# One matmul of 129 columns for the high and low values of three query tiles, a semaphore for each weight tile, and five high halves in eight on ScalarE

## What is computed

```
wp, wo = row-normalised w_proj (1536 x 512), w_out (512 x 512), over sqrt(512)
h = wp @ x                                   # 1024 x 1536: per head q, k, v
q, k = pixnorm(q) * s, pixnorm(k) * s; v = pixnorm(v)
attn = softmax(q k^T over the 1024 keys)     # per head 1024 x 1024
res = attn @ v
out = (0.7 * x + 0.3 * (wo @ res)) / sqrt(0.58)
```

## Time and profile before

| | |
|---|---|
| median of 3 runs | 2988.52 us |
| the profiled execution, its own time | 2986.36 us |
| its span, first to last instruction | 2984.6 us |
| TensorE busy | 2933.4 us, 36928 matmuls |
| VectorE busy | 2581.7 us |
| ScalarE busy | 2383.4 us |
| GpSimd busy | 454.9 us |
| mean granted TensorE clock | 0.999 of full speed |

### The profile page before, as it was taken

The page is one execution under the profiler, slowest core; times in us unless marked ns, Lnnn a source line. Parts: engine busy times, 40 slices in busy tenths (PEclk is TensorE's granted clock), DMA queues, the critical chain, the costliest instruction groups (busy, mean ns, idle before and its releaser), DMA issues.

```text
span 2984.6 us, 85445 instructions
## 1 busy us (share of the span) xinstructions
PE 2933.4 (98%) x36928; PEld 2013.6 (67%) x36928; DVE 2581.7 (87%) x3197; ACT 2383.4 (80%) x2993; POOL 454.9 (15%) x678
## 2 busy tenths in 40 slices
PE   7999999999999999999999999999999999999998
PEld 5776666766667667676666766667666666666765
DVE  6898888988889888898888988888888888988887
ACT  6887878878778778787787877878787787878786
POOL 0210121101211112112111111012110121101210
PEclk9999999999999999999999999999999999999999
DMA  3133414333242332333323333223323334334234
GB/s 106 41 56 63 91 36 108 51 79 79 44 97 50 81 78 48 90 62 76 72 52 85 62 79 69 65 72 62 85 63 69 76 54 96 60 63 86 40 80 103
DMA packets 459529, 211.04 MB, mean 71 GB/s; under 512 B 407952, under 2 KB 407952, under 8 KB 459152
## 3 DMA queue, kind: packets, MB, share of 16 engines
q1 hardware_dynamic: 459152, 205.58, 32.3%
HBM read 71.30 MB, written 33.55 MB: 35 GB/s over the span
## 4 chain that ended last, share of the span: by engine, by line
PE 79%; DVE 8%; POOL 5%; ACT 3%; DMA 3%; issue 2%; SPq 0%; ACTq 0%; DVEq 0%
PE ps_pv L973 21%; PE ps_score L952 19%; PE ps_dense L930 11%; PE ps_dense L932 10%; PE ps_dense L934 10%; DVE probs L780 4%; PE ps_dense L989 3%; PE ps_dense L990 2%; PE ps_dense L991 2%; DMA x_raw<-in_x 2%; POOL rs_t L442 1%; POOL rs_t L444 1%; POOL rs_t L446 1%; ACT e_tile L596 1%; DVE probs L771 1%
## 5 line engine op out<-in xcount | busy, mean ns | idle before, releaser
L780 DVE TENSOR_TENSOR probs<-e_tile,probs 128x1024 f16<-128x1024 f32 x1024 | 1241.4, 1230 | 64.6 <-ACT probs L603 58.7
L596 ACT ACTIVATE e_tile<-ps_score,shift 128x1024 f32<-128x1024 f32 x1024 | 1107.9, 1118 | 223.7 <-PE ps_score L952 130.2
L973 PEld LDWEIGHTS ps_pv<-v_pair,probs 128*128 128x128 f16 x24576 | 772.2, 98 | 183.5 <-issue 112.4
L973 PE MATMUL ps_pv<-v_pair,probs 128*128 128x65 f16 (+1 forms) x24576 | 821.6, 193 | 2.9 <-DVE probs L780 1.7
L952 PE MATMUL ps_score<-qkT 64*128 64x512 f16 x6144 | 753.4, 378 | 3.3 <-ACT e_tile L596 3.1
L930 PE MATMUL ps_dense<-wpT_hi,x_hi 128*128 128x512 f32 x1536 | 621.0, 404 | 2.4 <-DVE wpT_lo L851 2.3
L932 PE MATMUL ps_dense<-wpT_lo,x_hi 128*128 128x512 f32 x1536 | 600.1, 391 | 0.0
L934 PE MATMUL ps_dense<-wpT_hi,x_lo 128*128 128x512 f32 x1536 | 599.0, 390 | 0.0
L603 ACT ACTIVATE probs<-e_tile 128x1024 f16<-128x1024 f32 x512 | 542.8, 1061 | 22.8 <-PE ps_pv L973 4.0
L952 PEld LDWEIGHTS ps_score<-qkT 64*128 64x128 f16 x6144 | 257.0, 94 | 361.4 <-issue 90.2
L771 DVE CAST probs<-e_tile 128x1024 f16<-128x1024 f32 x512 | 360.0, 703 | 72.0 <-PE ps_pv L973 67.6
(11 more groups left out here) (50 smaller groups left out, 1739.4 us busy)
## 6 DMA issues: line engine op xcount, KB each, us to landing
x_raw<-in_x SPq DMA_DIRECT2D x128, 256.0 KB, 3.4
x_res<-in_x SPq DMA_DIRECT2D x128, 256.0 KB, 3.6
out<-x_res SPq DMA_DIRECT2D x128, 256.0 KB, 2.5
arena<-in_w_proj SPq DMA_DIRECT2D x24, 128.0 KB, 2.9
qkT<-arena SPq DMA_TRANSPOSE x128, 4.8
resT<-res_split SPq DMA_TRANSPOSE x128, 3.6
arena<-in_w_out SPq DMA_DIRECT2D x1, 1024.0 KB, 8.0
```

The lines of the kernel that those rows point to most:

```text
L596: act.activation(e_tile[:, t % E_BUFS, :, :], ps_score[:, t % 2, :, :], ACT.Exp, bias=shift[:, 0:1], scale=1.0 / (QK_UP * QK_UP)).then_inc ...
L780: dve.tensor_tensor(probs_of(b, t, 1), e_tile[:, t % E_BUFS, :, :], probs_of(b, t, 0), ALU.subtract).then_inc(probs_low, 1)
L973: mm = pe.matmul(ps_pv[:, h, o:o + n], probs_of(b, t, part)[:, h, queries], v[:, cols], start=(j == 0 and it == 0 and part == 0 and cols.s ...
```

## The change

- In `attend`, the values of a key tile now lie as 64 low columns, 64 high ones and the ones column. For query tiles 1 to 3 one matmul of 129 columns with the high probabilities writes low and high products side by side in `ps_pv` (129 columns a tile), and the low probabilities' product of 65 columns adds to the high part. Query tile 0 is as before, three matmuls into 65 columns.
- `take_pv` multiplies the high parts (3 x 64 columns for two heads, 384 elements), the low parts (384) and tile 0 (128), after which `pv_taken` is raised, and then adds the low parts to the others in SBUF and raises `res_made`, for which `high_res` waits.
- Each of the 12 projection weight tiles has a semaphore and a place in the tables of its own; the square waits for its own tile's two DMAs. The output weights are still one DMA.
- `ACT_HIGH` is (1, 2, 3, 5, 7).
- All three sets of tables are new; for the start, those of the weights and x loads among them.

```diff
-ACT_HIGH = (1, 3, 5, 7)
+ACT_HIGH = (1, 2, 3, 5, 7)
...
-    "W_LOAD_AT": (12240, 12288, 12336, 12384),
+    "LOAD_X_AT": (17680, 17728, 17792, 17808, 17872, 17920, 17952, 18000),
+    "W_LOAD_AT": (17696, 17712, 17744, 17760, 17776, 17824, 17840, 17856, 17888, 17904, 17936, 17968, 17984),
...
         SUMS = D + 1
-        LOW = D + 8
+        HIGH = D
+        BOTH = HIGH + SUMS
+        QUERIES = 4
...
+        res_low_part = sb("res_low_part", [P, 2, QUERIES - 1, D], F32)
...
-            def load_weights(g):
+            def load_weights(m):
...
+                p, kind = LAYOUT[m]
+                for h in range(2):
+                    sp.dma_start(w_raw[h * D:(h + 1) * D, m, :],
+                                 wp_in[2 * p + h, WEIGHT_ROWS[kind], :, :]).then_inc(w_loaded[m], 16)
...
-                act.wait_ge(w_loaded[m // 4], 16 * (8 if m < WP_TILES else 1))
+                act.wait_ge(w_loaded[min(m, WP_TILES)], 16 * (2 if m < WP_TILES else 1))
...
-                act.wait_ge(pv_taken, UNITS * b + u + 1)
+                act.wait_ge(res_made, UNITS * b + u + 1)
...
                 dve.wait_ge(pv_inverted, done + 1)
-                dve.tensor_tensor(res[:, u % 2, :, :].rearrange("p i (h d) -> p h i d", d=D),
-                                  sums[:, :, :, 0:D],
-                                  inv_sum[:, u % 2, :, :].unsqueeze(3).broadcast_to([P, 2, 4, D]),
+                dve.tensor_tensor(made[:, :, 1:, :], parts[:, :, :, HIGH:HIGH + D], whole[:, :, 1:, :],
+                                  ALU.mult).then_inc(pv_scaled, 1)
+                dve.tensor_tensor(res_low_part[:, :, :, :], parts[:, :, :, 0:D], whole[:, :, 1:, :],
+                                  ALU.mult).then_inc(pv_scaled, 1)
+                dve.tensor_tensor(made[:, :, 0, :], ps_pv[:, :, 0:D], whole[:, :, 0, :],
                                   ALU.mult).then_inc(pv_taken, 1)
+                dve.wait_ge(pv_scaled, 2 * done + 2)
+                dve.tensor_tensor(made[:, :, 1:, :], made[:, :, 1:, :], res_low_part[:, :, :, :],
+                                  ALU.add).then_inc(res_made, 1)
...
-                            for part, cols in ((0, slice(0, SUMS)), (0, slice(LOW, LOW + D)), (1, slice(0, SUMS))):
+                            products = ((0, high, o), (0, low, o), (1, high, o)) if it == 0 else                                        ((0, both, o - HIGH), (1, high, o))
+                            for part, cols, at_col in products:
                                 n = cols.stop - cols.start
```

More of the change, by code:

```diff
@@ new lines @@
+    "HIGH_V_AT": (-5936, -32, 112, 432, 29600, 31344, 37136, 38560),
+    "LOW_V_AT": (-432, -224, 0, 3360, 33312, 33344, 39600, 49568),
+    "TURN_QK_AT": (-11680, -10480, 21248, 26624, 30704, 45472, 51744, 51792),
+    "HIGH_QK_AT": (-15376, -5296, 11280, 14080, 14144, 19040, 29936, 37264),
+    "LOW_QK_AT": (-5744, -192, 12112, 14848, 19584, 21824, 39488, 48528),
+    "TAKE_AT": (14432, 21856, 26512, 35584, 45952, 59504, 64912, 67184),
+    "TURN_RES_AT": (44384, 47376, 51760, 51776, 54752, 82784, 84416, 92000),
@@ new lines @@
+    "HIGH_RES_AT": (14256, 21232, 29088, 40496, 43072, 49824, 59136, 70320),
+    "LOW_RES_AT": (21904, 26448, 26720, 48832, 57296, 65072, 65136, 69632),
+    "OUT_AT": (77472, 82928, 83472, 89984, 98128, 99728, 109344, 110160),
+    "ADD_OUT_AT": (69408, 77824, 79872, 87552, 92096, 92352, 103744, 104976),
+    "FINISH_AT": (76384, 79168, 86640, 90112, 92496, 102640, 107776, 114144),
+    "LOAD_X_AT": (-47504, -39040, -38896, -38880, -36688, -27008, -20704, -20048),
+    "HIGH_X_AT": (-51264, -51136, -44336, -42112, -40928, -39120, -37216, -34256),
@@ L153 @@
+    "LOW_X_AT": (-50608, -45680, -41024, -39440, -38992, -38928, -38832, -30512),
+    "LOAD_RES_AT": (55040, 55088, 92016, 92208, 104224, 110464, 111056, 111728),
+    "STORE_AT": (90432, 92048, 103840, 105872, 110672, 111040, 117936, 120464),
+    "PROJ_BANK": (0, 1, 0, 1, 0, 1, 0, 1, 0, 1, 0, 1, 0, 1, 0, 1, 1, 0, 1, 0, 1, 0, 0, 1),
     "OUT_BANK": (0, 1, 0, 1, 0, 1, 0, 1),
@@ new lines @@
+    "TURN_QK_AT": (18016, 19640, 21248, 26624, 30704, 45472, 51744, 51792),
+    "HIGH_QK_AT": (13488, 13568, 14128, 14256, 14343, 16432, 29936, 37264),
+    "LOW_QK_AT": (14224, 14304, 14800, 15632, 17744, 21824, 39488, 48528),
+    "TAKE_AT": (14752, 21856, 26512, 35584, 45952, 59504, 64912, 67184),
+    "TURN_RES_AT": (44384, 47376, 51760, 51776, 54752, 82784, 84416, 92000),
+    "HIGH_RES_AT": (14224, 21232, 29088, 40496, 43072, 49824, 59136, 70320),
+    "LOW_RES_AT": (21904, 26448, 26720, 48832, 57296, 65072, 65136, 69632),
@@ new lines @@
+    "TURN_QK_AT": (-10552, 18064, 30549, 34426, 44980, 45084, 45688, 45856),
+    "HIGH_QK_AT": (-13275, -6072, 13458, 19236, 19703, 23881, 26573, 26831),
+    "LOW_QK_AT": (-3160, -45, 15104, 18944, 20096, 21632, 27765, 38593),
+    "TAKE_AT": (11657, 20480, 26127, 29664, 38747, 39552, 39744, 39952),
+    "TURN_RES_AT": (45032, 45512, 46024, 48261, 50330, 53242, 54960, 55024),
+    "HIGH_RES_AT": (13284, 24640, 26508, 40185, 48624, 48848, 48928, 49072),
+    "LOW_RES_AT": (12697, 23314, 26747, 39132, 39664, 39728, 39776, 39984),
@@ new lines @@
+    "OUT_AT": (45072, 45120, 45136, 45152, 45168, 45184, 45200, 45216),
+    "ADD_OUT_AT": (39936, 39968, 40000, 40016, 40032, 40048, 40064, 40080),
+    "FINISH_AT": (49056, 49088, 49104, 49120, 49136, 49152, 49168, 49184),
+    "LOAD_X_AT": (-76768, -76000, -38888, -36848, -27040, -26024, -20880, -20504),
+    "HIGH_X_AT": (-51336, -49816, -44888, -40952, -40928, -39280, -37796, -28406),
+    "LOW_X_AT": (-48976, -47520, -41112, -39480, -39072, -38856, -29942, -28856),
+    "LOAD_RES_AT": (54085, 54944, 55008, 55040, 55088, 55104, 55152, 55168),
@@ L348, in prepare_and_attend @@
         ps_dense = pb("ps_dense", [P, 2, NH], F32)
-        w_loaded = [sem(f"w_loaded{g}") for g in range(W_GROUPS)]
+        w_loaded = [sem(f"w_loaded{m}") for m in range(WP_TILES + 1)]
         ident_made = sem("ident_made")
@@ L528, in task @@
             def task(b, s, when):
-                for g in when["w_load"].get(s, ()):
-                    load_weights(g)
+                for m in when["w_load"].get(s, ()):
+                    load_weights(m)
                 for piece in when["load_x"].get(s, ()):
@@ L574, in high_v @@
                 heads = slice(2 * (p % 2), 2 * (p % 2) + 2)
-                act.activation(v_pair[:, heads, half * HALF_NT:(half + 1) * HALF_NT, 0:D]
+                act.activation(v_pair[:, heads, half * HALF_NT:(half + 1) * HALF_NT, HIGH:HIGH + D]
                                .rearrange("p h n d -> p n h d"),
@@ L967, in attend @@
                         v = v_pair[:, 2 * (p % 2) + h, j, :]
-                        for it in range(4):
+                        high, low, both = slice(HIGH, HIGH + SUMS), slice(0, D), slice(0, BOTH)
+                        for it in range(QUERIES):
                             queries = slice(it * P, (it + 1) * P)
-                            o = it * SUMS
-                            for part, cols in ((0, slice(0, SUMS)), (0, slice(LOW, LOW + D)), (1, slice(0, SUMS))):
+                            o = it * BOTH
+                            products = ((0, high, o), (0, low, o), (1, high, o)) if it == 0 else                                        ((0, both, o - HIGH), (1, high, o))
+                            for part, cols, at_col in products:
                                 n = cols.stop - cols.start
-                                mm = pe.matmul(ps_pv[:, h, o:o + n], probs_of(b, t, part)[:, h, queries], v[:, cols],
-                                               start=(j == 0 and it == 0 and part == 0 and cols.start == 0),
+                                mm = pe.matmul(ps_pv[:, h, at_col:at_col + n], probs_of(b, t, part)[:, h, queries],
+                                               v[:, cols], start=(j == 0 and it == 0 and part == 0 and cols is high),
                                                stop=(j == UNIT_SLOTS - 1), skip_group_check=True)
```

226 lines of the change are left out of this document (93 added, 133 removed), and 72 rows, old and new, of tables (FIRST, LAST, STEADY).

## The result

The changed kernel took 3038.83 us (median of 5 runs, 3031.53 to 3043.22), beside 2988.01 us of the kernel before in the same session (5 runs, 2987.12 to 2990.43): a ratio of 1.0165 [1.0153, 1.0177]. The prediction said 2969. The profiled execution took 3035.28 us, with a span of 3033.5, which is 48.9 us more than the span before.

The account below looks back on a forecast made before the run. TensorE's own work was taken to bound the middle, VectorE the last 75 us. Terms -20.6 - 3 + 4 = -19.6 took the profiled 2986.4 to 2966.8; with 2.1 for the median, 2969 us, range 2943 to 2985.

Parts of the forecast that it names:

- The middle's waits: Mid-run waits under the new lists of order: counted as 0, between -15 and +15 us.
- The rival for the slower side: First value step of each unit: accumulator's release becomes the wait, 0.71 us a unit; 3012 to 3033 us; chance 0.08.
- rival (b): Fuller VectorE and ScalarE cost TensorE about one more 1.2 us wait an image: +19, 2988 us; chance 0.12.
- The take: Accumulator's take on VectorE: 1.27 us longer, +162 us for VectorE, release 0.71 us later; costed at nothing in the middle.
- Merging: Value matmuls: 6 fewer a key tile, 3.5 ns each over 980 key tiles, -20.6 us.
- The far end of 45 us: Value matmuls: those that remain get cheaper too, gain 45 us instead of 21, so 2945 us; chance 0.25.
- The start: Start of the run: squares wait only for their own transfers, chain near 10.6 us; -3 us, between 0 and -5.
- Engines: Whole run: VectorE becomes 2654 and ScalarE 2519 us busy, both staying under TensorE.
- The last stretch: Last some 6 units, where VectorE sets the pace without cover: +4 us, between 2 and 8.

Follow-up runs that it names:

- the best version: The changed kernel with banks of projection tiles 0 and 1 exchanged and store 2 and residual load 4 earlier in the sync queue: 2965.14 us, ratio 0.9920.

## Why the prediction was wrong, by its own steps

**The middle's waits.** This step failed: "All lists of order are new", and I took 0, between -15 and +15, by looking at waits that would go. Those did go (18 us of standing, more than thought). What the new order would bring was not followed. The runs show +55 us of waits in one place an image and +21 of low clock. All that was needed stood in the change: projection tile 0 comes directly after output step 4, both have bank 0, and the store that the add's residual depends on comes in the sync queue after a transpose of 3 us. Exchanging two bank numbers gives 55 us back, and moving the store too gives 74.

**The rival for the slower side** was a wait at the value accumulator; it was 7.6 us, as before. Its direction and its size (3012 to 3033) were near, by chance: the place and the mechanism were other ones. Nor did rival (b) hold: the waits of weight loads for low halves, which were to double, are 40.3 us in place of 42.6.

**The take, "at nothing in the middle, under the cover of 13% idle VectorE".** The reason was wrong, even if the number stood. Under the old order the take costs 52 us and 1.26 us of work behind it 67, through the low halves queued there. In the new order the waits for low halves are as before, so it costs little there; that this is so because the order was made for it isn't shown, since no run has the new order with the old take. A part is the fifth high half, which leaves the queue: without that, 39 us. The price of an edit and the price of the edit with its order differ by more than the whole gain. So the parts can't be summed: old order, take and merging give +38, and the complete change with the fault mended -23.

**Merging.** Right in mechanism, a little smaller: 707 ns a key tile in place of 725, 3.0 ns for each removed matmul against the 3.5 taken, 18 us against 20.6. A group of 36 lasts 1.41 us (1456.26 to 1457.67), foretold 1.42. The far end of 45 us is excluded. The Trainium skill (TensorE: Matmul & The Clock Gate, Back-to-back issue gap) has two rules that bear on it. By its 81 ns for a sustained pair of load and matmul of 128 columns, the twelve matmuls of 129 columns in a group would need 0.97 of its 1.41 us and leave the other 24 only 18 ns each, less than their 64 or 65 columns are at 2.4 GHz (27 ns); the trace disagrees. By the page's N/2.4 + 2.5 the 36, of 86 columns on average, would take 38.4 ns each: the trace has 39.2, 0.8 over that rule, where it was 1.0 over before.

**The start.** Right: the norm chain began at 10.57, foretold 10.6, TensorE's first work at 14.80 in place of 16.56, and projection at 19.69 in place of 22.74, foretold near 20: the 3 us that were taken. That the separate semaphores are worth 7 us in the best version doesn't contradict it: there the group wait meets the new order of loads, in which a group's last tile comes later than it did before.

**Engines.** VectorE 2637 for 2654, ScalarE 2480 for 2519: right that neither becomes the bound. **The last stretch**, +4, was about right: by the starts in the traces, 115.4 us pass before from the first value matmul of the last six units to the end, 118.9 after and 120.2 in the best version. In the version with both entries mended, the sum of the prediction's terms comes true (2965 for 2969), though some of that is one error against another: merging brings 18 and not 20.6, and the standing of matmuls after the first one falls by 5 us (28.3 to 22.9) where 0 was taken.

## What to carry over

When an order changes, follow every shared buffer through it: who filled it last, who empties it, and back from there to the DMA that this one needs and its place in the issuing queue; a few table entries turned a gain of 23 us into a loss of 51. An idle share of 13% is no cover to count on in a queue that is worked off strictly in order: of 161 us put there 67 came through. What counts is which operation stands behind the new one, and who waits for it. And undo the order and the edit separately, since each may be worthless or harmful without the other.

## What was not expected of the hardware

- After 12 of the 13 waits of 3.2 to 4.9 us TensorE's granted clock was down at 1.2 GHz for about 3 us (0.42 us in place of 0.23 for an fp32r matmul of 512 columns), in two of them for longer. The length of the wait alone doesn't decide: behind one of 3.43 us the clock stayed up, and with the store moved it fell behind 7 of 12 waits of 2.4 us and not behind one of 3.5. What else decides stays open here. The mean clock was 0.992, 0.996 with most waits at 2.4 us, 0.999 with none over 2.5.
- An fp32r projection matmul behind an output matmul in float16 costs nothing beside its columns (0.45 us for the two), though the list shows 0.42 us to the next; one behind value matmuls costs 0.09 us more than within its group.
- GpSimd took 1543 ns for an add of 384 elements that VectorE does in 548, and slowed VectorE's own two-operand operations meanwhile: those of 1024 elements took 1576 ns beside such an add and 1218 beside nothing.
- A transpose DMA held the sync queue for 3.16 us at its issue (1801.48), an ordinary load for 0.33.
